# Broadcasts of two kinds of reciprocal deviations in rows of 4 and 2 KB, and x's tiles 4 to 7 loaded in pairs

## The reference

```
x = x + conv_recurrence(ln_over_channels(x))        # eps 1e-6
    fs  = masked 3x1 conv of the normalized x, 256 gate channels   (taps: row above, row here)
    for each of the 32 rows j:
        i, g, f, o = split(conv3(h, w_stos) + b + fs[row j])
        c_new = sigmoid(f) * c + sigmoid(i) * tanh(g)
        h_new = c * sigmoid(o)                       # row j of the result
t = tokens of x  (16 x 1024 x 64)
t = t + moe(ln(t))                                   # eps 1e-5
    probs = softmax over the 1024 tokens of logits(32 experts); the 8 best tokens per expert
    pooled -> gelu(pooled W1) W2 -> added to the picked tokens
```

## Time and profile before

| | us |
|---|---|
| median of 3 runs | 209.29 |
| lowest, highest | 209.09, 210.82 |
| the profiled execution, whole | 208.52 |
| its span | 206.7 |
| PE busy | 178.4 (86%) |
| DVE busy | 165.5 (80%) |
| POOL busy | 125.4 (61%) |
| ACT busy | 109.3 (53%) |

### The profile page before, as it was taken

How to read it: one execution, slowest core, us unless ns; L and a number is a source line. 1 busy time by engine, 2 the same in 40 slices (tenths; PEclk the granted TensorE clock), 3 DMA queues, 4 the chain that set the end, 5 groups by cost and what they waited for, 6 DMA issues and landing times.

```text
span 206.7 us, 10869 instructions
## 1 busy us (share of the span) xinstructions
PE 178.4 (86%) x4687; PEld 146.7 (71%) x4687; DVE 165.5 (80%) x605; ACT 109.3 (53%) x266; POOL 125.4 (61%) x113
## 2 busy tenths in 40 slices
PE   1689987989998999999999999999997997998900
PEld 1479866889877877987897898898784776684200
DVE  0778797989895999999889977987889999445960
ACT  2373526566652664665556577566557696640000
POOL 4454369598885989798598979759338931000000
PEclk9999999999999999999999999999999999999975
DMA  4955140910551092056131103100399960000896
GB/s 114 172 111 108 36 77 5 182 29 6 126 88 53 11 200 60 5 110 101 54 88 40 46 6 105 54 8 3 103 232 218 199 127 0 3 6 9 230 350 227
DMA packets 28992, 19.12 MB, mean 93 GB/s; under 512 B 2336, under 2 KB 27920, under 8 KB 28944
## 3 DMA queue, kind: packets, MB, share of 16 engines
q1 hardware_dynamic: 27312, 15.87, 36.0%
q10 hardware_dynamic: 1632, 2.56, 4.1%
HBM read 14.12 MB, written 4.30 MB: 89 GB/s over the span
## 4 chain that ended last, share of the span: by engine, by line
PE 49%; DVE 25%; DMA 7%; issue 6%; POOL 4%; ACT 3%; SPq 2%; DVEq 0%; POOLq 0%
PE ps L939 33%; PE ps L930 7%; PE ps L999 3%; DVE ps L708 3%; POOL r L397 3%; DVE st L667 3%; DMA w_rows<-in_L_conv_w_stos 3%; DMA scratch<-r1t 2%; DVE tail_room L923 2%; DVE xtok L923 2%; DVE lg L864 2%; DVE x_split L859 2%; DMA rbf<-scratch 2%; DVE fc L711 1%; DVE cands L853 1%
## 5 line engine op out<-in xcount | busy, mean ns | idle before, releaser
L939 PE MATMUL ps<-x_split,w_hi 64*64 64x256 f16 x1000 | 50.2, 273 | 2.9 <-DVE fc L711 1.9
L375 POOL TENSOR_TENSOR xc<-xc,h 128x256 f32<-128x256 f32 x31 | 22.5, 724 | 24.6 <-DVE h_lo L692 24.6
L939 PEld LDWEIGHTS ps<-x_split,w_hi 64*64 64x64 f16 x1000 | 25.5, 106 | 15.0 <-issue 8.5
L939 PE MATMUL ps<-h_hi,w_lo 64*64 64x256 f16 x750 | 32.3, 272 | 0.7 <-issue 0.7
L939 PE MATMUL ps<-h_lo,w_hi 64*64 64x256 f16 x750 | 32.3, 271 | 0.5 <-issue 0.5
L708 DVE TENSOR_TENSOR ps<-sg_i,ps 64x256 f32<-64x256 f32 x62 | 26.7, 430 | 7.4 <-ACT ps L508 5.8
L939 PE MATMUL ps<-h_hi,w_hi 64*64 64x256 f16 x750 | 31.9, 271 | 0.0
L492 ACT ACTIVATE ps<-ps,bias 128x256 f32<-128x256 f32 x32 | 14.3, 448 | 32.4 <-PE ps L939 32.3
L397 POOL TENSOR_TENSOR r<-v,pow_exp 128x16 f32<-128x16 f32 x7 | 20.5, 2935 | 8.6 <-DVE v L661 8.6
L930 PE MATMUL ps<-ident,xc 128*128 128x128 f32 x128 | 18.5, 288 | 7.4 <-DMA xc<-in_x 5.8
L939 PE MATMUL ps<-x_split,w_lo 64*64 64x256 f16 x500 | 24.7, 269 | 0.0
(11 more groups left out here) (130 smaller groups left out, 328.6 us busy)
## 6 DMA issues: line engine op xcount, KB each, us to landing
xc<-in_x SPq DMA_DIRECT2D x14, 256.0 KB, 5.7
rb_xr<-scratch SPq DMA_DIRECT2D x14, 256.0 KB, 4.4
w1s<-in_L_ffn_weight SPq DMA_DIRECT2D x4, 512.0 KB, 10.7
w2s<-in_L_ffn_weight SPq DMA_DIRECT2D x4, 512.0 KB, 10.7
rbf<-scratch SPq DMA_DIRECT2D x24, 64.0 KB, 2.2
out<-xtok SPq DMA_DIRECT2D x4, 256.0 KB, 5.4
out<-xtok ACTq DMA_DIRECT2D x4, 256.0 KB, 5.9
out<-tail_room SPq DMA_DIRECT2D x3, 256.0 KB, 4.4
```

The source lines that it names most:

```text
L375: p.tensor_tensor(here, here, h32[:, i % 2, :].rearrange("p (b w) -> p b w", w=W), ALU.add) \
L939: ins = pe.matmul(pre[gate][to, 0:COLS], w[half(h), tap, C * GATE_ORDER[gate]:][:, 0:C], data[half(h)], start=first and m == 0, stop=s_don ...
```

## The change

1. The first deviations are kept by half: POOL writes column (h, b) of `r0` from column (b, h) of the variances. After the turn, the 8 rows of one half of the images lie together in `scratch0`, and each of the two broadcasts reads one run of 1024 elements (4 KB) per partition in place of 8 runs of 512 bytes.
2. The second deviations are kept by quarter (`by_image`): column (q, g) from column (g, q). Each of the four broadcasts reads one run of 512 elements (2 KB) per partition in place of 4 runs. `scale_tokens` and PE's `spread` for the last tile read the columns in the new order. The parts of the last tile's power (`LAST_R`) are now given in groups, with the same number of columns: 4, 4 and 8.
3. x's tiles 4 and 5 are loaded together at t = 0, tiles 6 and 7 together at t = 2, in runs of 1 KB; no x is loaded at t = 1 and t = 3. PE waits on the pair's semaphore (`x_load`).
4. The issue of the experts' weights is written as a loop over pairs; its order is the same.

```diff
-LAST_R = slice(0, 4), slice(4, 8), slice(8, 16)
+LAST_R = slice(0, 1), slice(1, 2), slice(2, 4)
@@
+def x_load(u):
+
+    return u if u < 4 else u // 2 * 2
@@ SyncE
-            def load_x(u, halves):
-                for h in halves:
-                    q.dma_start(xc[half(h), :, u, :], x_cm[h, :, :, u * TOK:u * TOK + TOK]).then_inc(s_x[u], DMA)
...
+            def load_x(u, count=1):
+                for h in range(2):
+                    q.dma_start(xc[half(h), :, u:u + count, :].rearrange("p b t k -> p b (t k)"),
+                                x_cm[h, :, :, u * TOK:(u + count) * TOK]).then_inc(s_x[u], DMA)
@@ spread_r0
-                    q.dma_start(rb[half(h), :, :], scratch0[u % 2].rearrange("(b h) t -> h b t", h=2)[h]
+                    q.dma_start(rb_xr[half(h), 0, :], scratch0[u % 2].rearrange("(h b) t -> h (b t)", h=2)[h]
                                 .partition_broadcast(C)).then_inc(s_rb_in, DMA)
@@ spread_r1
-                r_g = scratch1.rearrange("(g q) t -> q g t", q=QUAD)
+                r_g = scratch1.rearrange("(q g) t -> q (g t)", q=QUAD)
                 for k in range(QUAD):
-                    q.dma_start(rbf[E * k:E * k + E, :, :], r_g[k].partition_broadcast(E)).then_inc(s_rbf_in, DMA)
+                    q.dma_start(rbf[E * k:E * k + E, :, :].rearrange("p g t -> p (g t)"), r_g[k].partition_broadcast(E)) \
+                        .then_inc(s_rbf_in, DMA)
@@ the loop over tiles
-                if t < 4:
-                    load_later(t)
+                if t in (0, 2):
+                    load_x(4 + t, 2)
@@ GpSimd
-                p.tensor_tensor(r0[:, u % 2, :], v0[:, 3, :], pow_exp[:, :], ALU.pow).then_inc(s_r0, 1)
+                p.tensor_tensor(r0[:, u % 2, :].rearrange("p (h b) -> p b h", h=2), v0[:, 3, :].rearrange("p (b h) -> p b h", h=2),
+                                pow_exp[:, :].rearrange("p (b h) -> p b h", h=2), ALU.pow).then_inc(s_r0, 1)
+
+            def by_image(r):
+
+                return r.rearrange("p (q g) -> p g q", q=QUAD)
...
-                p.tensor_tensor(r1[:, u % 2, :], v1[:, 3, :], pow_exp[:, :], ALU.pow).then_inc(s_r1, 1)
+                p.tensor_tensor(by_image(r1[:, u % 2, :]), v1[:, 3, :].rearrange("p (g q) -> p g q", q=QUAD),
+                                pow_exp[:, :].rearrange("p (g q) -> p g q", q=QUAD), ALU.pow).then_inc(s_r1, 1)
...
-                here = xtok[:, u, 8 * k:8 * k + 8, :]
-                p.tensor_tensor(here, here, r1[:, u % 2, 8 * k:8 * k + 8].unsqueeze(2).to_broadcast([128, 8, C]),
+                here = xtok[:, u, 8 * k:8 * k + 8, :].rearrange("p (g q) c -> p g q c", q=QUAD)
+                p.tensor_tensor(here, here, by_image(r1[:, u % 2, :])[:, 2 * k:2 * k + 2, :].unsqueeze(3).to_broadcast([128, 2, QUAD, C]),
                                 ALU.mult).then_inc(s_xtok_scaled, 1)
@@ TensorE
-                    pe.wait_ge(s_x[t + AHEAD], 2 * DMA)
+                    pe.wait_ge(s_x[x_load(t + AHEAD)], 2 * DMA)
...
-                    c = QUAD * g + q
+                    c = QUAD * q + g
```

More of the change, by code:

```diff
@@ L278, in _, with load_experts @@
         def _(q):
-            def load_x(u, halves):
-                for h in halves:
-                    q.dma_start(xc[half(h), :, u, :], x_cm[h, :, :, u * TOK:u * TOK + TOK]).then_inc(s_x[u], DMA)
[L283 to L288, removed]
-                some = slice(E // 4 * m, E // 4 * m + E // 4)
[L290 to L295, removed]
+            def load_x(u, count=1):
+                for h in range(2):
+                    q.dma_start(xc[half(h), :, u:u + count, :].rearrange("p b t k -> p b (t k)"),
+                                x_cm[h, :, :, u * TOK:(u + count) * TOK]).then_inc(s_x[u], DMA)
+            def load_experts(m):
+                some = slice(E // 4 * m, E // 4 * m + E // 4)
+                q.dma_start(w1s[half(m % 2), E // 4 * (m // 2):E // 4 * (m // 2) + E // 4, :],
+                            w1[some, 0:C, :].rearrange("e c h -> c e h")).then_inc(s_expert_w_in, DMA)
+                q.dma_start(w2s[:, some, :, :], w2[some, 0:H, :].rearrange("e (j k) o -> j e k o", k=2)) \
+                    .then_inc(s_expert_w_in, DMA)
             def spread_r0(u):
@@ L319, in _ @@
                 q.dma_start(w_rows[:, 0, n, :], w[0:128].rearrange("o c k one -> o (c k one)")).then_inc(s_conv_w_in, DMA)
-            load_x(1, (0, 1))
+            load_x(1)
             for h in range(2):
@@ L326, in _ @@
                     q.dma_start(b_rows[:, n, half(h)], b.rearrange("(g c) -> g c", c=C)).then_inc(s_bias_in, DMA)
-            load_x(2, (0, 1))
+            load_x(2)
             q.wait_ge(s_gate_zeroed, 1)
@@ L335, in _ @@
                 q.dma_start(b1_rows[E * k:E * k + E // 4, :], w1[E // 4 * k:E // 4 * k + E // 4, C, :]).then_inc(s_b1_in, DMA)
-            load_x(3, (0, 1))
+            load_x(3)
             spread_r0(1)
@@ L342, in _ @@
                     spread_r0(t + 2)
-                if t < 4:
-                    load_later(t)
-            for n in range(4, 12):
-                load_later(n)
+                if t in (0, 2):
+                    load_x(4 + t, 2)
+            for m in range(4):
+                load_experts(m)
             for n, part in enumerate(FIRST_PARTS):
@@ L457, in _ @@
                     p.memset(pool_t[:, :, :], 0.0).then_inc(s_pool_room, 1)
-            for n, part in enumerate(LAST_R):
+            for n, groups in enumerate(LAST_R):
                 p.wait_ge(s_x1_var, 4 * NT + (0 if n < 2 else 4))
-                p.tensor_tensor(r1[:, (NT - 1) % 2, part], v1[:, 3, part], pow_exp[:, part], ALU.pow).then_inc(s_r1, 1)
+                p.tensor_tensor(by_image(r1[:, (NT - 1) % 2, :])[:, groups, :], v1[:, 3, :].rearrange("p (g q) -> p g q", q=QUAD)[:, groups, :],
+                                pow_exp[:, :].rearrange("p (g q) -> p g q", q=QUAD)[:, groups, :], ALU.pow).then_inc(s_r1, 1)
             for k in range(2):
```

## The result

The changed kernel takes 211.66 us (median of 6 runs, 210.22 to 213.25); the kernel before takes 208.98 us in the 6 runs beside it (206.05 to 210.82). The ratio is 1.018, with a 95% interval of 1.009 to 1.027. A ratio here is one of means, and an execution that took over 1.5% longer than its kernel's fastest is left out of it (here two of the six of before), so it can differ from that of the medians (here 1.013). The forecast was 207.7 us, range 206.0 to 209.6: the time lies outside it, on the other side.

A forecast was written before the change was run, and what follows sets the result against it. PE was taken to bound tiles 1 to 5, so only its idle moments could be won: -1.04 - 0.3 - 0.46 + 0.2 = -1.6 us, from the median 209.29 to 207.7 us, range 206.0 to 209.6.

The forecast's parts named there:

- No load of x at t = 1: Tile 2: store of `r1t` lands at least 2.65 us earlier, DVE's 2.46 us wait goes, PE gains 1.04 us.
- I leave it: 0 (... +0.7 if the doubled load brings a second one): PE's 0.70 us idle at 44.80, after tile 4's load: unchanged, 0; bounds -0.70 and +0.7.
- Together 6.2 in place of 5.3 ... : 0: Tile 3: broadcasts 1.5 plus x pair 4.7 us; `rbf` 0.9 us later, absorbed, so 0 for PE.
- the output's 341 GB/s: Rate of the output's 4 KB rows, taken for the broadcasts in 4 KB rows, giving 1.5 us.
- bound of 8.0 us: Tile 3: upper bound for broadcasts plus x pair if all moves at 197 GB/s, 2.7 us late.
- +1.3: Tile 3: PE's cost in us if `rbf` comes 2.7 us late, less 1.4 absorbed.
- the 1.4 taken: About 1.4 us of DVE's lateness is absorbed without cost to PE: 2.46 less 1.04.
- rival B: Longer runs are not quicker, all at 197 GB/s; tile 3 pays 1.3 us, sum 0: 209.3 us, chance 0.15.
- The 0.46 at 95.61: PE's "issue" idle at the end of tile 7's load goes without a load at t = 3: -0.46 us.
- The 0.54 at 77.97: PE's wait for DVE's fc, after DVE's stall, falls from 0.54 to 0.22: -0.3 us.
- The powers, +0.2: POOL's power `rsqrt0` gains 7 rows at 0.025 us each; PE waits for it at 30.90: +0.2 us.
- rival D: POOL starts anew for every short row of a power, `rsqrt0` 2.5 us dearer: +5.6, 214.9 us, chance 0.08.

The follow-up runs named there:

- 2 MB kernel: Kernel before with x loaded in spaced single tiles, tile 4 after the first broadcasts, plus 2 MB of experts' weights issued in tile 6: 211.07 us, ratio 1.017.
- 1 MB kernel: Kernel before with x loaded in spaced single tiles, tile 4 after the first broadcasts, plus 1 MB of experts' weights issued in tile 6: 207.7 us, ratio 0.997.
- experiment 3, spaced: Kernel before with single x loads: tile 4 unmoved, tile 5 ahead of t = 1's broadcasts, 6 and 7 right behind the `rbf` broadcasts: 206.07 us, ratio 0.991.
- experiment 5: Changed kernel with only the pair of x tiles 6 and 7 moved, to right behind tile 2's `rbf` broadcasts: median 212.94 us, ratio 1.011.

## Why the prediction was wrong

**No load of x at t = 1: right, and larger.** The store of `r1t` of tile 2 landed in 1.35 us, DVE did not wait, and tile 2 gave 1.87 us where 1.04 was forecast: 1.10 of idle time, as forecast, and 0.77 of busy time, which I had not counted. PE's busy time was longer in the tile in which DVE waited for `rbf` (17.96 with the wait, 17.19 without, for the same matmuls), and tile 3 of after pays the same the other way round, with 18.03 for 17.40 before. A stop of PE alone does not do it: tile 1 of after, with 3.40 us of it, has 16.35 for 16.26. Why is open.

**"I leave it: 0 (... +0.7 if the doubled load brings a second one)": the step that failed first.** It measured +2.70. I had read the 0.70 us at 44.80 as an idle moment without a cause and scaled it with the number of loads. It is a late instruction packet, and its price goes by how late the packet is against PE's reaching the same place in its program: the packet at 42.0 cost 0.70, that at 45.0 cost 3.40. So the term was no second idle of the same size, but the same one, longer by the whole delay of the packet.

**"Together 6.2 in place of 5.3 ... : 0": the second.** Two broadcasts and a load took 5.3 us in before; with a pair in place of the load they took 8 in after the first time and 9 the second. Windows of after (first three) and then of before (last), columns as in rows 2; the third and the fourth are a pair of broadcasts with nothing beside it:

```profile
37.50:45.50 8.00, 6.94 (x220) 6.40 (x209) 7.19 (x34) 5.08 (x12) 5.73 (x6) 1.00 0.91 199
73.30:82.30 9.00, 8.97 (x253) 7.19 (x245) 8.73 (x35) 5.72 (x14) 7.97 (x7) 1.00 0.87 179
112.90:115.15 2.25, 2.22 (x75) 1.82 (x69) 2.21 (x9) 0.99 (x3) 2.25 (x3) 1.00 0.89 224
```

```profile
106.65:109.15 2.50, 2.47 (x85) 2.08 (x77) 2.00 (x6) 1.46 (x4) 2.50 (x3) 1.00 0.83 207
```

A pair of broadcasts takes 2.25 us in 4 KB rows and 2.5 in 512-byte runs, a tenth less, where I had taken 1.5 us from the output's 341 GB/s. The pair of x moves at 179 to 199 GB/s with its broadcasts, not at 225. So my bound of 8.0 us "at 197 for all of it" was near the truth and its price of 2.7 us late was nearly met (3.0). But +1.3 was too small a price. The same transfers also held back PE's own instructions: PE stood for 1.78 us inside DVE's 5.28 and for 1.83 behind them, so that 5.28 - 1.78 - 1.83 = 1.67 us were absorbed, near the 1.4 taken. Tile 3 paid for both: 3.61 of idle time in these rows, against 0.54 before. The rule on 512 bytes of the Trainium skill ("DMA: Bandwidth & Descriptors", Specifications), which rival B followed, is the nearer one: the measured gain beyond 512 bytes is a tenth. Output is a transfer to DRAM in another stretch, and was the wrong row to price a load by.

**The 0.46 at 95.61: right in number, not shown in reason.** No "issue" idle stands in tile 4 of after. But in the 2 MB kernel, which loads tile 7 at 75.65, long before, and has only broadcasts there, an idle of 0.46 stands at 92.78, at the same place of PE's program (number 4488). That it went with the load was in part luck. **The 0.54 at 77.97: wrong for its place.** An idle of 0.56 stands at 100.94 now, one tile later, again in the tile that follows the stall of DVE. It belongs to the lateness, which moved, and is not gone.

**The powers, +0.2: wrong, 0.012.** 2947 ns against 2935 for 8 rows of 2, 1082 against 1068 for the scaling. With this rival D is refuted. The 0.95 us at 30.90 even fell to 0.30, but PE had an "issue" idle of 0.74 at 25.46 before it, so that the start of tile 1 was no earlier (38.81 against 38.47).

**The rivals.** None was right. B had the transfers right (no quicker) and put the time at 209.3, since it priced only the broadcast's lateness. D, the one slower rival of any size, was built on POOL, when the change's plain cost was 0.5 MB more on the DMA engines at once; a case in which the doubled load costs more than DVE's wait, with a term for the unnamed idle, was missing. The check that would have found it was in the page of before: 37 packets of instructions; and in the trace, none of them between 35.5 and 42 us, where tile 4 was loaded, with the "issue" idle of the earlier trace rows right behind it.

## What to carry to other kernels

Before you merge transfers, add up what is queued on the DMA engines at once: here two broadcasts and one load, 1 MB, cost PE 0 to 0.7 us of late instructions, and 1.25 to 2 MB cost 0.7 to 3.4, though PE waited for none of the data. A long unrolled program on PE needs its own instructions from the same DMA engines, one packet of 16 KB every 4.3 us, and an idle of PE that is released by "issue" behind a burst should be checked against the packets of its instruction queue; space loads so that they fill the gaps between broadcasts, and don't count on another queue to keep a small transfer quick. Runs longer than 512 bytes made these broadcasts a tenth quicker, which does not pay for a burst.

## What the hardware showed that I had not expected

- **Instruction packets wait behind bulk,** with the gaps and idle times of the table, whichever engine issues the bulk, and PE stops for them only at the end of a packet's 253 instructions.
- **A store behind one broadcast pair on its queue** took 7.11 us with the pair of x on another queue, nearly the 7.66 that it took with all of them on one; in tile 2 of after, without bulk, it took 1.35.
- **The clock can make it dearer.** In the 2 MB kernel the granted clock stood at 1.00, the level of 2.4 GHz, until PE's idle of 3.41 us, and at 0.50, that of 1.2 GHz, in the 6 us behind it (windows, clock third from the right):

```profile
136.00:138.00 2.00, 0.00 (x0) 0.00 (x0) 0.82 (x3) 0.42 (x1) 2.00 (x1) 0.96 1.16 192
138.00:140.00 2.00, 1.03 (x21) 1.03 (x24) 0.00 (x0) 0.00 (x0) 2.00 (x4) 0.50 0.73 181
140.00:142.00 2.00, 2.00 (x47) 2.00 (x42) 0.00 (x0) 0.22 (x1) 1.84 (x2) 0.50 0.06 16
142.00:144.00 2.00, 2.00 (x44) 2.00 (x40) 1.60 (x5) 0.59 (x2) 0.00 (x0) 0.50 0.00 0
```

  Tile 6 takes 22.73 us there and 16.40 without the bulk: 3.4 of the 6.3 us are the idle, the rest lies at the lower clock. In after an idle of the same length (3.40 us at 47.84) left the clock at 1.00 in every window around it, and in the 1 MB kernel one of only 2.02 us is followed by 0.50 (140.0 to 142.0). So the length of the idle alone does not decide it, and why they differ is open.
- **Left open:** how long a bulk holds a packet back (one passes at 75.0 in after, some 3 us after two broadcasts were issued, and none at 36.5 to 45), and why some come late with little bulk near, as behind the 0.3 to 0.5 us of "issue" that wander between the kernels. Each trace is one execution, and runs of one kernel differ by up to 6.1 us (experiment 3, spaced: 203.72 to 209.81), in experiment 5 by far more.
